# Attention of an adaLN layer with experts: q and k in two float32r parts, heads two by two in the halves of TensorE

## The chip, the cores and the metric

The kernel runs on one core of one Trainium2 chip. The metric is the device time of one execution in microseconds. TensorE is PE, its weight loads PEld, VectorE is DVE, ScalarE ACT, GpSimd POOL; SP issues most DMAs.

## The reference

One transformer layer on x of 2048 tokens by 256 numbers, float32. `sa, ca, ga, sb, cb, gb` are rows of 256 made from a vector c; of the experts only the sizes matter here.

```python
h = layernorm(x) * (1 + ca) + sa
qkv = h @ w_qkv.T + b_qkv                      # 16 heads of 16 numbers
scores = q @ k.T / 4 + causal                  # per head 2048 x 2048
out = softmax(scores) @ v
x = x + ga * (out @ w_out.T + b_out)
h = layernorm(x) * (1 + cb) + sb
x = x + gb * ffn(h)                            # top 1 of 8 experts, at most 320 tokens each, 256 -> 1024 -> 256
```

## The kernel before

**Tiles.** The 16 heads are four groups of four (g), the 2048 queries four blocks of 512 (b); n = 4 g + b counts 16 blocks. For each block the kernel needs the row maxima of the scores first, and then the transposed scores (keys by queries), whose exponentials are the weights of the values. So each product of q and k is formed twice. *Maxima*: for one head, one tile of 128 queries and one chunk of up to 512 keys a matmul (L1295) writes a PSUM bank and DVE reduces it (L1049); in the chunk with the diagonal DVE adds the causal mask and reduces in one instruction (L1055). *Scores*: for one head and one tile of 128 keys a matmul (L1325) writes 128 keys by up to 512 queries and ACT takes the exponential (L802). For the tiles on the diagonal only the later queries are formed (512, 384, 256 or 128 columns) and POOL zeroes the triangle (L698). *Weigh* (L1245): four heads' values by the exponentials of one tile of keys, float32, each head in its own 32 columns of the array, added up in one bank. A *step* here is one tile of keys: scores of its four heads, maxima of blocks to come, and the weigh of the tile before it; 160 steps in all.

**Precision.** q and k are float32 numbers split in three bfloat16 parts (L757, L762 on ACT, `leave_part0` and `leave_part1` on DVE or POOL). The six products that matter stand below each other in `stacks`: 6 x 16 = 96 rows. Eight more rows carry minus the row maximum in two bfloat16 parts (q side) and ones for the own head, zeros for the others (k side), so that the score matmul of 104 rows gives score minus maximum. The parts go through DRAM (`qk_rows`) to be laid out so: `store_parts` (six DMAs for a block) and `load_stacks` (two DMAs), all issued by SP in a fixed order. The projections of a group (L1187, float32, in four pieces) run between the steps of the group before; group 0 is made in the prologue.

**Maxima rows.** When the last maxima of a block are read, DVE forms the two parts (`max_parts`), PE turns them (L1302), ACT copies the eight rows to the first head's stack (L790) and signals (L793), and DVE copies them to the three others (L1075). The first score of the block waits for that.

**Order.** Each engine runs its instructions in order. `attention_plan` writes one list of events for all of them, with a clock of its own that says when a bank is free. Maxima use banks 0 to 2 in turn, scores banks 3 to 5, the weigh bank 6, everything else bank 7: a maxima matmul waits for the read three before it, a score for the exponential three before it:

```python
                    if u >= 3:
                        pe.wait_ge(max_read, u - 2)
                    q0 = b * QB + qt * P
```

When no maxima are left, steps of the output projection, second layernorm and gate for the first 12 token tiles (`tail_slot`) are put between the scores of the last two blocks.

## Time and profile before

| | |
|---|---|
| three runs | 782.13, 784.63, 785.97 us |
| median | 784.63 us |
| span of the profiled execution | 782.6 us, mean granted clock 0.943 |
| PE, DVE, ACT, POOL busy | 88, 72, 59, 17% |
| maxima, 640 matmuls | 197.7 us busy on PE |
| scores, 640 matmuls | 195.4 us busy on PE |
| weigh, 1280 matmul records | 151.6 us busy on PE |
| exponentials, 640 | 298.3 us busy on ACT |
| maxima read without and with mask, 384 and 256 | 250.7 and 120.7 us busy on DVE |

The page names one time for the profiled execution, its span. The time of a run is taken from the device and not from the trace. L numbers are lines of the kernel before. The busy time of PE is made of modelled ends, so matmuls that follow each other overlap in it. A float32 matmul stands in the trace as two records, one of bfloat16 or float32r as one. All events of attention lie before 594 us of the span; then come the last four token tiles, the scatter of the tokens to their experts and, from 633 us, the experts.

### The profile page before, as it was taken

To read this page: it belongs to the slowest core of one execution; us is meant where nothing else is said; L and a number is where in the kernel's file an instruction comes from. 1 tells how busy PE (TensorE), PEld (TensorE's weight loads), DVE (VectorE), ACT (ScalarE), POOL (GpSimd) and SP (SyncE) were. 2 spreads that over 40 slices of the span, in tenths; PEclk is the share of its full clock that TensorE was granted. 3 is DMA by queue.
4 is the path that set the end of the run, shared out by engine and by line. 5 is a ranking of instruction groups with operands and counts; after the bars stand their busy time and mean duration, and the time that the engine had idled before them with its cause. 6 is when DMAs were issued, how large, how long until landed. Compare 5 with 4: busy or idle time off the path is not lost.

```text
span 782.6 us, 12208 instructions
## 1 busy us (share of the span) xinstructions
PE 689.1 (88%) x4290; PEld 367.2 (47%) x4290; DVE 561.1 (72%) x1467; ACT 459.5 (59%) x962; POOL 133.9 (17%) x194
## 2 busy tenths in 40 slices
PE   4686989999999998999999999989996279999994
PEld 3564534432323343323332323242543269999994
DVE  7754778788888787988888898960435437777762
ACT  1422445566676667766677676657783336656551
POOL 6000222220001132003310201100105300121122
PEclk9869889999999999999999999999999559999998
DMA  7436126630006033005900006000004283455200
GB/s 243 109 76 144 41 57 147 162 68 14 2 0 162 1 81 81 2 1 124 308 1 1 1 1 214 1 28 1 28 28 162 90 234 115 155 182 201 92 23 17
DMA packets 42111, 66.53 MB, mean 85 GB/s; under 512 B 3822, under 2 KB 31985, under 8 KB 41466
## 3 DMA queue, kind: packets, MB, share of 16 engines
q1 hardware_dynamic: 39746, 59.44, 27.3%
q0 software_dynamic: 2304, 6.31, 2.2%
q8 instruction: 34, 0.56, 0.3%
q14 instruction: 27, 0.22, 0.1%
HBM read 39.36 MB, written 26.78 MB: 85 GB/s over the span
## 4 chain that ended last, share of the span: by engine, by line
PE 74%; DVE 10%; ACT 8%; issue 4%; DMA 2%; POOL 1%; SPq 0%; DVEq 0%; POOLq 0%; ACTq 0%
PE bank L1245 17%; PE bank L1295 15%; PE bank L1325 14%; PE bank L1430 9%; PE bank L1413 8%; ACT probs L802 4%; PE bank L1187 3%; DVE chunk_max L1049 2%; PE bank L1350 2%; PE bank L1216 1%; PE bank L1396 1%; ACT qk_sb L751 1%; PE bank L1373 1%; PE bank L1228 1%; DVE stats L907 1%
## 5 line engine op out<-in xcount | busy, mean ns | idle before, releaser
L802 ACT ACTIVATE probs<-bank 128x512 f32<-128x512 f32 (+3 forms) x640 | 298.3, 537 | 124.1 <-PE bank L1325 123.0
L1049 DVE TENSOR_REDUCE chunk_max<-bank 128x1 f32<-128x512 f32 x384 | 250.7, 685 | 36.9 <-PE bank L1295 35.9
L1325 PE MATMUL bank<-stacks 104*128 104x512 bf16 (+3 forms) x640 | 195.4, 356 | 13.5 <-ACT probs L802 10.1
L1295 PE MATMUL bank<-stacks 96*128 96x512 bf16 (+3 forms) x640 | 197.7, 359 | 7.9 <-DVE chunk_max L1049 3.2
L1245 PE MATMUL bank<-probs,v_sb 128*32 128x512 f32 (+3 forms) x1280 | 151.6, 546 | 0.1
L1055 DVE CUSTOM_DVE_ANT_0 masked<-bank,causal 128x128 bf16<-128x128 f32 (+3 forms) x256 | 120.7, 484 | 15.4 <-PE bank L1295 14.6
L1295 PEld LDWEIGHTS bank<-stacks 96*128 96x128 bf16 x640 | 56.0, 98 | 160.0 <-DVE chunk_max L1049 79.4
L698 POOL TENSOR_SCALAR_AFFINE_SELECT probs<-probs 128x512 f32<-128x512 f32 x64 | 40.6, 635 | 397.4 <-ACT probs L802 397.4
L1325 PEld LDWEIGHTS bank<-stacks 104*128 104x128 bf16 x640 | 62.2, 100 | 98.7 <-ACT probs L802 65.6
L1430 PE MATMUL bank<-w_split,acts 128*128 128x256 f32 x576 | 79.9, 284 | 0.0
L1430 PEld LDWEIGHTS bank<-w_split,acts 128*128 128x128 f32 x576 | 74.5, 190 | 1.5 <-issue 0.8
L1413 PE MATMUL bank<-slotT,w_split 128*128 128x320 f32 x384 | 70.0, 320 | 2.1 <-DVE slotT L1109 2.1
L1413 PEld LDWEIGHTS bank<-slotT,w_split 128*128 128x128 f32 x384 | 59.5, 196 | 3.1 <-issue 2.3
L862 ACT ACTIVATE acts<-bank 128x320 fp32r<-128x320 f32 x64 | 28.0, 438 | 55.4 <-PE bank L1413 55.4
L1139 DVE TENSOR_TENSOR acts<-act_raw,acts 128x320 fp32r<-128x320 f32 x64 | 31.4, 490 | 33.6 <-ACT act_raw L865 33.6
L1187 PEld LDWEIGHTS bank<-hT,w_qk_sb 128*128 128x128 f32 x256 | 40.7, 219 | 13.8 <-issue 9.1
L1098 DVE TENSOR_TENSOR w_split<-w_raw,w_split 128x1024 fp32r<-128x1024 f32 x32 | 38.9, 1224 | 10.6 <-ACT w_split L837 10.6
L731 POOL DMA_INDIRECT out<-down,slots_sb x24 | 23.6, 984 | 132.0 <-DVE down L1127 127.2
L1187 PE MATMUL bank<-hT,w_qk_sb 128*128 128x128 f32 x256 | 43.7, 309 | 2.7 <-ACT hT L771 2.7
L1245 PEld LDWEIGHTS bank<-probs,v_sb 128*32 128x32 f32 x1280 | 25.4, 108 | 44.0 <-issue 27.6
L751 ACT ACTIVATE qk_sb<-bank,b_qk_sb,qk_scale 128x512 f32<-128x512 f32 x16 | 12.4, 777 | 43.2 <-PE bank L1187 43.2
L837 ACT CAST w_split<-w_raw 128x1024 fp32r<-128x1024 f32 x32 | 33.3, 1049 | 0.0
(140 smaller groups left out, 533.6 us busy)
## 6 DMA issues: line engine op xcount, KB each, us to landing
stacks<-qk_rows SPq DMA_DIRECT2D x6, 1536.0 KB, 12.4
w_raw<-w_in SPq DMA_DIRECT2D x8, 1024.0 KB, 5.0
w_raw<-w_down SPq DMA_DIRECT2D x8, 1024.0 KB, 8.0
qk_rows<-part SPq DMA_DIRECT2D x32, 192.0 KB, 2.9
slot_rows<-empty SPq DMA_DIRECT2D x1, 5140.0 KB, 28.9
slots_sb<-slot_rows SPq DMA_DIRECT2D x8, 514.0 KB, 4.0
qk_rows<-part SPq DMA_DIRECT2D x32, 128.0 KB, 2.4
stacks<-qk_rows SPq DMA_DIRECT2D x8, 384.0 KB, 4.5
```

Of the source, the lines that this page charges most:

```text
L698: pool.affine_select(out=d, in_=d, compare_op=ALU.is_ge, fill=0.0, base=0, pattern=[[0, HG], [1, P]], channel_multiplier=-1).then_inc(diag ...
L802: act.activation(probs[:, s % 3, h, 0:width], bank[SCORE_BANKS[u % 3]][:, 0:width], ACT.Exp)\
L837: act.copy(chunk(w_split[e % 2][:, 0, :], c), chunk(w_raw[:, e % 2, :], c)).then_inc(w_high, 1)
L1049: dve.tensor_reduce(to, src[:, 0:QB], AX.X, ALU.max).then_inc(max_read, 1)
L1055: dve.tensor_tensor_reduce(out=masked[:, u % 3, 0:width], in0=src[:, 0:width], in1=causal[:, QB - width:QB], scale=1.0, scalar=NEG, op0=AL ...
L1098: dve.tensor_tensor(chunk(w_split[e % 2][:, 1, :], c), chunk(w_raw[:, e % 2, :], c), chunk(w_split[e % 2][:, 0, :], c).bitcast(F32), ALU.s ...
L1187: mm = pe.matmul(bank[MISC_BANK][:, at:at + width], w_qk_sb[:, k, g * P:(g + 1) * P], hT[:, k, b * QB + at:b * QB + at + width], start=(k ...
L1245: mm = pe.matmul(bank[VALUE_BANK][CT * h:CT * (h + 1), lo:QB], v_sb[:, kt, g * HG + h, :], probs[:, s % 3, h, 0:QB - lo], start=first, sto ...
L1295: pe.matmul(bank[MAX_BANKS[u % 3]][:, 0:width], stack(g, 0)[0:KR, h, q0:q0 + P], stack(g, 1)[0:KR, h, c * QB:c * QB + width], start=True, ...
L1325: pe.matmul(bank[SCORE_BANKS[u % 3]][:, 0:QB - lo], stack(g, 1)[0:KR + MR, h, kt * P:(kt + 1) * P], stack(g, 0)[0:KR + MR, h, b * QB + lo: ...
L1413: mm = pe.matmul(bank[n % 3][:, 0:CAP], w_split[e % 2][:, a, col:col + P], slotT[:, e % 2, b, k, :], start=(i == 0 and k == 0), stop=(i == ...
L1430: mm = pe.matmul(bank[DOWN_BANKS[st]][:, 0:D], acts[:, n % AR, a, st * P:(st + 1) * P], w_split[e % 2][:, b, col:col + D], start=(it == 0 ...
```

## The change

q and k are split in two float32r parts instead of three bfloat16 ones, three products instead of six: 48 rows, 56 with the maxima rows. Two heads then fit in the array, one in rows 0 to 63 and one in rows 64 to 127. Each event of maxima or scores is now a pair of heads: two matmuls, one in each half, into the two banks of one of three buffers, and one instruction of DVE or ACT that reads 128 x 2 x up to 512 numbers. Maxima and scores share the three buffers; the plan gives each event the buffer that its own clock has free first, and the event waits for the last reader of that buffer, whichever kind it was (`free_pair`). In the first block's maxima only buffer 0 is used. When no maxima are left, scores use buffers 1 and 2, and the tail work of the first 12 tiles banks 0 and 1 only. The causal mask is added on PE: four short bfloat16 matmuls (a shifted identity by a shifted mask) ahead of the pair. The maxima rows are copied by ACT to a buffer of their own and from there by two DMAs, issued by SP, to both halves of the array's rows; SP's order now follows the plan. The ones rows (k side), before four ACT instructions of 8 x 2048 (L780) and a DMA, are eight DMAs at the start. ACT rounds the high part straight from PSUM, and one subtraction gives the low part. Stores of parts are four DMAs for a block, loads four; their bytes are the same. The experts are untouched.

```diff
-PARTS_Q = [0, 0, 0, 1, 1, 2]
-PARTS_K = [0, 1, 2, 0, 1, 0]
+PARTS_Q = [0, 0, 1]
+PARTS_K = [1, 0, 0]
 KR = HD * len(PARTS_Q)
+HALF = P // 2
+PAIRS_OF_HEADS = HG // 2
 MR = 2 * HG
...
-    return [[(qt, h, c) for qt in range(TB) for h in range(HG) for c in range(b + 1)] for b in range(NB)]
+    return [[(qt, j, c) for qt in range(TB) for j in range(PAIRS_OF_HEADS) for c in range(b + 1)] for b in range(NB)]
...
+    def usable():
+
+        if not started:
+            return [0]
+        return [0, 1, 2] if count < len(maxima) else [1, 2]
+
+    def next_buffer():
+        return min(usable(), key=lambda i: free_at[i])
...
+        i = next_buffer()
+        plan.append(("max", count, g, b, qt, j, c, width, i))
+        tensor(width / TENSOR_RATE + (50 if c < b else 130), free_at[i])
+        vector = max(vector, now + READ_LATENCY) + 2 * width / VECTOR_RATE + VECTOR_FIXED
+        free_at[i] = vector + FREE_LATENCY
+        count += 1
...
+    freed_by = {}
+    held = [None, None, None]
+    exps = 0
+    for ev in plan:
+        if ev[0] == "max":
+            freed_by[ev] = held[ev[-1]]
+            held[ev[-1]] = ("max_read", ev[1] + 1)
+        if ev[0] == "scores":
+            exps += 1
+            freed_by[ev] = held[ev[-1]]
+            held[ev[-1]] = ("exp_done", exps)
+    exps_of_first = held[0]
...
+        pair_bank = [ctx.enter_context(nc.psum_tensor(f"pair{i}", [P, 2, QB], F32)) for i in range(4)]
+        bank = [pair_bank[i // 2][:, i % 2, :] for i in range(8)]
...
-        stacks = sb1("stacks", [P, 2, 2, HG, S], BF16)
+        stacks = sb1("stacks", [P, 2, 2, PAIRS_OF_HEADS, S], F32R)
...
-        STACK_DMAS = 2
-        STORES = 6
+        STACK_DMAS = 4
+        STORES = 4
+        ROW_DMAS = 2
...
+            def load_group(g):
                 sp.wait_ge(parts_stored, 16 * STORES * NB * (g + 1))
                 if g >= 2:
 
-                    sp.wait_ge(scored, HG * (last_step[(g - 1) * NB - 1] + 1))
+                    sp.wait_ge(scored, 2 * (last_step[(g - 1) * NB - 1] + 1))
                 load_stacks(g, slice(0, S), stacked[g])
+
...
+            sp.wait_ge(heads_marked, 1)
+            for r in range(2):
+                for a in range(2):
+                    for j in range(PAIRS_OF_HEADS):
+                        marks = head_rows[:, a, j, :].rearrange("p (c s) -> p c s", c=1)
+                        to = stacks[HALF * a + KR:HALF * a + KR + MR, r, 1, j, :].bitcast(F32)
+                        sp.dma_start(to.rearrange("p (c s) -> p c s", s=MARKS),
+                                     marks.broadcast_to([MR, S // MARKS, MARKS])).then_inc(ones_copied, 16)
+            stored, grouped = 0, 0
...
+                if ev[0] == "max_rows":
+                    n = ev[1]
+                    g, b = divmod(n, NB)
+                    sp.wait_ge(misc_read_a, misc_reads(misc_use[ev])[0] + 1)
+                    row = max_row[:, n % 2, :].bitcast(F32).rearrange("p (j s) -> p j s", j=1)
+                    for a in range(ROW_DMAS):
+                        rows = stack(g, 0)[HALF * a + KR:HALF * a + KR + MR, :, b * QB:(b + 1) * QB].bitcast(F32)
+                        sp.dma_start(rows, row.broadcast_to([MR, PAIRS_OF_HEADS, QB]))\
+                            .then_inc(max_rows[n % 2], 16)
...
+            eng.tensor_tensor(part[:, 1, :], qk_sb[:, :], part[:, 0, :].bitcast(F32), ALU.subtract).then_inc(done, 1)
...
                 act.activation(qk_sb[:, :], bank[MISC_BANK][:, :], ACT.Identity, bias=b_qk_sb[:, g:g + 1],
+                               scale=qk_scale[:, 0:1])
+                if n >= 1:
+
+                    act.wait_ge(parts_stored, 16 * STORES * n)
+                act.activation(part[:, 0, :], bank[MISC_BANK][:, :], ACT.Identity, bias=b_qk_sb[:, g:g + 1],
                                scale=qk_scale[:, 0:1]).then_inc(misc_read_a, 1)
                 act.wait_ge(misc_read_a, misc_reads(misc_use["project", g, b])[0] + 1)
-                if n >= 1:
-
-                    act.wait_ge(parts_stored, 16 * STORES * n)
-                act.copy(part[:, 0, :], qk_sb[:, :]).then_inc(part0_ready, 1)
-
...
-            def second_part(g, b):
-                n = g * NB + b
-                act.wait_ge(rest_ready_v if g == 0 else rest_ready_p, n + 1 if g == 0 else n + 1 - NB)
-                act.copy(part[:, 1, :], rest[:, :]).then_inc(part1_ready, 1)
...
-                    second_part(0, b)
-
-                    act.activation(stacks[KR:KR + MR, 0, 1, b, :], ones_b[KR:KR + MR, 0:1].broadcast_to([MR, S]),
-                                   ACT.Copy, scale=head_sel[KR:KR + MR, b:b + 1]).then_inc(ones_rows, 1)
...
-                    act.copy(stack(g, 0)[KR:KR + MR, 0, b * QB:(b + 1) * QB],
-                             bank[MISC_BANK][:, :].bitcast(BF16)[0:MR, 0:QB]).then_inc(misc_read_a, 1)
-                    act.wait_ge(misc_read_a, misc_reads(misc_use[ev])[0] + 1)
-                    act.copy(c_tmp[0:1, 1, 0:1], c_tmp[0:1, 0, 0:1]).then_inc(max_row0, 1)
+                    if n >= 2:
+
+                        act.wait_ge(max_rows[n % 2], 16 * ROW_DMAS * (n // 2))
+                    act.copy(max_row[:, n % 2, :], bank[MISC_BANK][:, :].bitcast(BF16)[0:MR, 0:QB])\
+                       .then_inc(misc_read_a, 1)
...
-                    act.activation(probs[:, s % 3, h, 0:width], bank[SCORE_BANKS[u % 3]][:, 0:width], ACT.Exp)\
+                    act.activation(probs[:, s % 3, 2 * j:2 * j + 2, 0:width], pair_bank[i][:, :, 0:width], ACT.Exp)\
...
-                        dve.tensor_reduce(to, src[:, 0:QB], AX.X, ALU.max).then_inc(max_read, 1)
-                    else:
-                        if u >= 3:
-                            dve.wait_ge(max_read, u - 2)
-                        if u == 0:
-                            dve.wait_ge(causal_ready, 1)
-                        dve.tensor_tensor_reduce(out=masked[:, u % 3, 0:width], in0=src[:, 0:width],
-                                                 in1=causal[:, QB - width:QB], scale=1.0, scalar=NEG, op0=ALU.add,
-                                                 op1=ALU.max, accum_out=to).then_inc(max_read, 1)
+                    dve.tensor_reduce(chunk_max[:, n % 2, first:first + 2, c], pair_bank[i][:, :, 0:width], AX.X, ALU.max)\
+                       .then_inc(max_read, 1)
                 if ev[0] == "max_parts":
...
-                    rows = stack(g, 0)[KR:KR + MR, :, b * QB:(b + 1) * QB]
-                    dve.wait_ge(max_row0, n + 1)
-                    dve.tensor_copy(rows[:, 1:HG, :], rows[:, 0:1, :].broadcast_to([MR, HG - 1, QB]))\
-                        .then_inc(max_rows, 1)
...
-                    if u >= 3:
-                        pe.wait_ge(max_read, u - 2)
+                    free_pair(ev)
                     q0 = b * QB + qt * P
-                    pe.matmul(bank[MAX_BANKS[u % 3]][:, 0:width], stack(g, 0)[0:KR, h, q0:q0 + P],
-                              stack(g, 1)[0:KR, h, c * QB:c * QB + width], start=True, stop=True).then_inc(max_scored, 1)
+                    if c == b:
+
+                        for at in (HALF, 0):
+                            for a in range(2):
+                                rows = slice(HALF * a, HALF * (a + 1))
+                                pe.matmul(pair_bank[i][:, a, width - P + HALF - at:width],
+                                          shifted_ident[rows, at:at + P], shifted_mask[rows, HALF:at + P],
+                                          start=(at > 0), stop=False, skip_group_check=True)
+                    for a in range(2):
+                        rows = slice(HALF * a, HALF * a + KR)
+                        mm = pe.matmul(pair_bank[i][:, a, 0:width], stack(g, 0)[rows, j, q0:q0 + P],
+                                       stack(g, 1)[rows, j, c * QB:c * QB + width], start=(c < b), stop=True,
+                                       skip_group_check=True)
+                    mm.then_inc(max_scored, 1)
...
-                    if u >= 3:
-                        pe.wait_ge(exp_done, u - 2)
-                    pe.matmul(bank[SCORE_BANKS[u % 3]][:, 0:QB - lo], stack(g, 1)[0:KR + MR, h, kt * P:(kt + 1) * P],
-                              stack(g, 0)[0:KR + MR, h, b * QB + lo:(b + 1) * QB], start=True, stop=True)\
-                        .then_inc(scored, 1)
+                            pe.wait_ge(ones_copied, 16 * 8)
+                    free_pair(ev)
+                    for a in range(2):
+                        rows = slice(HALF * a, HALF * a + KR + MR)
+                        mm = pe.matmul(pair_bank[i][:, a, 0:QB - lo], stack(g, 1)[rows, j, kt * P:(kt + 1) * P],
+                                       stack(g, 0)[rows, j, b * QB + lo:(b + 1) * QB], start=True, stop=True)
```

In the diff `freed_by[ev]` is the reader of the buffer that the event takes, found by going through the plan once.

The pieces of order below are of PE, in one and the same step late in block 7, from weigh to weigh. First before:

```order
L1295 MATMUL bank<-stacks 128x512 [waits max_read] x3
L1325 MATMUL bank<-stacks 128x512 [waits exp_done] x2
L1295 MATMUL bank<-stacks 128x512 [waits max_read]
L1325 MATMUL bank<-stacks 128x512 [waits exp_done] x2
L1295 MATMUL bank<-stacks 128x512 [waits max_read]
L1245 MATMUL bank<-probs,v_sb 32x512 [waits exp_done]
L1245 MATMUL bank<-probs,v_sb 32x512 x3
```

Then the same step in the changed kernel (L1388 scores, L1362 maxima, L1289 weigh):

```order
L1388 MATMUL pair<-stacks 128x512 [waits max_read]
L1388 MATMUL pair<-stacks 128x512
L1362 MATMUL pair<-stacks 128x512 [waits exp_done]
L1362 MATMUL pair<-stacks 128x512
L1388 MATMUL pair<-stacks 128x512 [waits max_read]
L1388 MATMUL pair<-stacks 128x512
L1362 MATMUL pair<-stacks 128x512 [waits exp_done]
L1362 MATMUL pair<-stacks 128x512
L1289 MATMUL pair<-probs,v_sb 32x512 [waits exp_done]
L1289 MATMUL pair<-probs,v_sb 32x512 x3
```

Five maxima and four scores have become two pairs of each, and every pair waits for a reader of the other kind.

The maxima rows on SP, in the changed kernel, around the load of group 2 (L668 maxima rows, L620 stacks, L608 and L613 stores of parts):

```order
L668 DMA stacks<-max_row 8x2x512 [waits misc_read_a]
L668 DMA stacks<-max_row 8x2x512
L668 DMA stacks<-max_row 8x2x512 [waits misc_read_a]
L668 DMA stacks<-max_row 8x2x512
L620 DMA stacks<-qk_rows 48x2x2048 [waits scored,parts_stored]
L620 DMA stacks<-qk_rows 48x2x2048 x3
L668 DMA stacks<-max_row 8x2x512 [waits misc_read_a]
L668 DMA stacks<-max_row 8x2x512
```

Before, the rows did not pass SP; on DVE the copy stood among the maxima reads (L1049, L1055):

```order
L1049 TENSOR_REDUCE chunk_max<-bank 128x1 [waits max_scored]
L1055 ISA masked,chunk_max<-bank,causal 128x128 [waits max_read,max_scored]
L1055 ISA chunk_max 128x1
L1075 COPY stacks<-stacks 8x3x512 [waits max_row0]
L1049 TENSOR_REDUCE chunk_max<-bank 128x1 [waits max_scored]
```

The copy has left DVE, and two DMAs of each block stand in SP's queue among loads and stores.

## Rows read from the trace of the kernel before

**Rows 1.** The page, part 1: busy us, share of the span, instructions.
```profile
PE 689.1 (88%) x4290; PEld 367.2 (47%) x4290; DVE 561.1 (72%) x1467; ACT 459.5 (59%) x962; POOL 133.9 (17%) x194
```

**Rows 2.** Stages: us, busy us (x) of PE, PEld, DVE, ACT, POOL, granted clock, DMA.
```profile
0.00:80.00 80.00, 52.14 (x232) 39.37 (x232) 48.67 (x172) 24.27 (x28) 12.39 (x47) 0.87 0.51 140
80.00:234.00 154.00, 143.88 (x841) 58.70 (x840) 127.16 (x333) 91.92 (x195) 28.49 (x32) 0.94 0.27 62
234.00:514.00 280.00, 268.30 (x1693) 93.08 (x1696) 242.30 (x619) 193.15 (x425) 47.66 (x68) 1.00 0.25 69
514.00:594.00 80.00, 72.81 (x468) 32.71 (x460) 29.00 (x117) 57.97 (x131) 5.93 (x9) 0.98 0.06 21
```

**Rows 3.** Waits, 80 to 516 us: us in total, times, longest.
```profile
ACT probs L802 <- PE bank L1325: 102.5, 118, 2.7
DVE chunk_max L1049 <- PE bank L1295: 35.9, 66, 2.8
```

**Rows 4.** Timeline (start us, us, engine): block 7, and one narrower weigh.
```profile
341.98 1.07 PE L1245 MATMUL bank<-probs,v_sb 128*32 128x512 f32 x8
...
345.19 1.07 PE L1245 MATMUL bank<-probs,v_sb 128*32 128x512 f32 x8
...
346.19 0.77 PE L1295 MATMUL bank<-stacks 96*128 96x384 bf16 x3
...
341.31 1.28 DVE L1049 TENSOR_REDUCE chunk_max<-bank 128x1 f32<-128x512 f32 x2
...
344.00 2.06 ACT L802 ACTIVATE probs<-bank 128x512 f32<-128x512 f32 x4 [1.03 <-PE bank L1325]
...
403.12 0.85 PE L1245 MATMUL bank<-probs,v_sb 128*32 128x384 f32 x8
```

**Rows 5.** Groups by form: xcount, busy us, mean ns of one, idle before.
```profile
L1049 DVE TENSOR_REDUCE chunk_max<-bank 128x1 f32<-128x512 f32 x384 | 250.7, 685 | 36.9 <-PE bank L1295 35.9
L802 ACT ACTIVATE probs<-bank 128x512 f32<-128x512 f32 x448 | 236.7, 602 | 95.1 <-PE bank L1325 94.3
...
L1055 DVE CUSTOM_DVE_ANT_0 masked<-bank,causal 128x256 bf16<-128x256 f32 x64 | 25.9, 417 | 3.7 <-PE bank L1295 3.6
...
L802 ACT ACTIVATE probs<-bank 128x256 f32<-128x256 f32 x64 | 20.2, 388 | 11.9 <-PE bank L1325 11.9
```

**Rows 6.** Timeline of the expert stage on PE, 660 to 664 us.
```profile
661.02 1.05 PE L1413 MATMUL bank<-slotT,w_split 128*128 128x320 f32 x6
...
662.96 1.05 PE L1413 MATMUL bank<-slotT,w_split 128*128 128x320 f32 x6
```

**Rows 7.** Timeline, 510 to 530 us: one score that ACT waited for.
```profile
511.66 0.38 PE L1325 MATMUL bank<-stacks 104*128 104x512 bf16 x1
...
512.08 0.60 ACT L802 ACTIVATE probs<-bank 128x512 f32<-128x512 f32 x1 [0.28 <-PE bank L1325]
```

**Rows 8.** Timeline of the prologue and of the first maxima rows.
```profile
56.48 1.99 ACT L780 ACTIVATE stacks<-ones_b,head_sel 8x2048 bf16<-8x2048 bf16 x1
...
78.30 0.57 ACT L790 COPY stacks<-bank 8x512 bf16<-8x512 bf16 x1 [11.39 <-PE bank L1302]
...
79.87 0.61 PE L1325 MATMUL bank<-stacks 104*128 104x512 bf16 x1 [0.54 <-DVE stacks L1075]
```

**Rows 9.** DMA issues: xcount, KB each, us to landing.
```profile
stacks<-qk_rows SPq DMA_DIRECT2D x6, 1536.0 KB, 12.4
...
qk_rows<-part SPq DMA_DIRECT2D x32, 64.0 KB, 2.5
```

**Rows 10.** Busy time in two short stretches of block 1, columns as in rows 2.
```profile
95.00:105.00 10.00, 7.20 (x34) 3.38 (x34) 9.26 (x25) 3.03 (x6) 1.15 (x1) 0.90 0.29 63
105.00:110.00 5.00, 5.00 (x25) 3.36 (x24) 2.45 (x6) 2.40 (x5) 1.78 (x2) 0.52 0.12 25
```

**Rows 11.** Timeline, PE, 540 to 550 us: two weighs in a row after the maxima.
```profile
543.25 1.06 PE L1245 MATMUL bank<-probs,v_sb 128*32 128x512 f32 x8
...
545.64 1.06 PE L1245 MATMUL bank<-probs,v_sb 128*32 128x512 f32 x8
```

305 lines of the change are left out of this document (165 added, 140 removed).

## The prediction

> **What bounds the kernel now.** The page's busy times come first [rows 1]: PE is busy for 88% of 782.6 us, DVE for 72%, ACT for 59%. That is an average, so the second view splits it by stage [rows 2]. The change touches only what lies before 594 us; the remaining 188.6 us (last tokens, experts) keep their instructions. From 80 to 514 us maxima and scores run beside each other: 154 us while the projections of two groups lie between them, then 280 us. There PE is busy for 93 to 96%, DVE for 83 to 87%, ACT for 60 to 69%. From 514 to 594 us no maxima are left. The third view is the waits [rows 3]: ACT waited 102.5 us for score matmuls, DVE only 35.9 us for maxima matmuls. The end of a matmul is modelled, so the fourth view is one step on the timeline [rows 4]. Weighs start at 341.98 and 345.19 us, a step of 3.21 us. The weigh holds PE until the next matmul at 346.19, 1.00 us; between weighs stand four scores and five maxima, nine matmuls of mostly 512 columns, each 213 ns at 2.4 GHz (granted 1.00): 1.92 us. PE streams 2.92 of 3.21 us. DVE is close behind: its 512-wide reads follow each other in 0.60 us, so five cost 3.0. ACT needs 2.06. So PE sets the step, and DVE would take over 0.2 us lower: halving PE's work cannot halve the time.
>
> **The new units.** 640 maxima become 320 pairs, 640 scores 320 pairs. Reading 1024 numbers at once: the 512-wide reduction takes 685 ns and 256 more columns cost 268 ns [rows 5], so alone it takes 685 + 536 = 1.22 us, and back to back 0.60 + 0.54 = 1.14 us, against 1.20 for two reads before. The exponential takes 602 ns at 512 and 388 at 256 [rows 5]: 602 + 428 = 1.03 us alone, and (2.06 - 0.60)/3 = 0.49 plus 0.43, 0.92 us, back to back.
>
> PE's price of a pair has no row, since no two row halves run at once before. The experts give a float32r matmul [rows 6]: six of 320 and nine of 256 columns in 1.94 us, where 4224 columns at 2.4 GHz are 1.76, so each costs its columns plus 12 ns. A pair of 512 columns then lies between 0.24 us (halves beside each other) and 0.45 us (one after the other). I take 0.25, as the weigh's rows are nearest: its eight records of 512 columns would be 1.71 us one after another even with one pass each, and took 1.00 [rows 4], so quarters of the array do run beside each other. That this holds for row halves in float32r is not shown.
> The Trainium skill (TensorE: Matmul & The Clock Gate, Part 3, packing small matmuls) has row tiles start about 4 ns apart; by it the pair is the lower bound, by its absence the sum below grows by the 48 us of the first rival.
>
> A diagonal maxima pair also gets its mask by four short bf16 matmuls, two by two: 192 columns, 80 ns; I take 0.1 us, 128 times, inside the steps.
>
> **The step after.** Three buffers serve both kinds, and a buffer is refilled only after its reader ends. From matmul start to ACT start is 0.42 us for 512 columns [rows 7], so the reader begins 0.21 us after the pair. In the order of block 7 (score, maxima, score, maxima, weigh) PE issues the score at 0, maxima at 0.25, score at 0.50, and the second maxima has to wait for the first score's buffer: 0.25 + 0.21 + 1.03 + 0.03 for the release = 1.52 (the 0.03 is my allowance). It ends at 1.77; the weigh (same four matmuls, 1.00 us) ends the step at **2.80 us** by rounding the buffer handover up. DVE's two reads need 2.3 of it. With a third maxima between, DVE is the limit of one read, and I take **3.0 us**. The same step before had 4.5 to 5 maxima.
>
> *234 to 514 us* (by the order 94 steps, blocks 4 to 13 and two of block 14). 60 full steps without projection, 44 with at most two maxima and 16 with more: 44 x 2.80 + 16 x 3.0 = 171. Four with a projection carry maxima of 18 full widths, which DVE reads in 18 x 1.14 = 21. Ten steps each of 384, 256 and 128 columns: 2.5, 2.1 and 1.5 us by the same walk, 61, less 13 because the weigh that follows is narrower. Heads out and turned, ten times 0.6: 6. Sum **246**, before 280: **-34**.
> *80 to 234 us* (39 steps): 22 full, 14 x 2.80 + 8 x 3.0 = 63; eight with a projection, maxima of 46 widths x 1.14 = 53; nine narrow ones 17 less 4; heads 4, and 4 for the rows of block 1, which come right before its first score: **137**, before 154: **-17**. Here PE's 1.7 us of a projection hides under DVE.
> *514 to 594 us*: scores have two buffers, ACT reads continuously: two exponentials back to back, 1.86 us, plus 0.1, against 2.39 [rows 11], for eleven plain steps: -5. The other steps carry the transposes, projections and gates of twelve token tiles; two pairs cost 0.5 us where four matmuls cost 0.85, for 13 steps -5, and the shared banks of the tail (0 and 1 only) give nothing back because DVE was waited for there anyway. **-10**.
> *Prologue*: four ACT instructions of 1.99 us that stood ahead of the next block's hT leave [rows 8], and one subtraction and one cast per block: about -6 on the path. The first eight maxima pairs now share one buffer, so PE and DVE alternate: 2 x (0.95 + 1.2 + 1.55 + 1.95) = 11.3 us against 5.6: +6. Maxima rows: before, ACT's copy starts at 78.30 and the first score at 79.87; now ACT's copy (0.57) is followed by two DMA issues on SP (0.6 each) and a landing of 2.5 us, the smallest store's [rows 9]: 4.3 instead of 1.6 us, +1 here since three maxima cover the rest. Later blocks are scheduled several us ahead. **+1**.
> SP's queue: rows stand behind stores and behind a 3 MB load whose halves land after 12.4 us [rows 9]. By the order at least eight score pairs, some 10 us, lie between them where they meet: nothing on the path. DVE's row copies and accumulator reads leave too; both are inside the read times above. POOL keeps one subtraction of two, off the path.
>
> Sum: 782.6 - 34 - 17 - 10 + 1 = 722.6. A stretch in which PE is paced by DVE lost clock before [rows 10]: granted 0.52 after ten us with PE busy for 72%. Five us at half clock delay PE by 2.5; with fewer columns I expect two such stretches more and add 5: **728 us**. The sum stands against the execution's 782.6; the median, 784.6, is 0.3% above, which is nothing beside the terms.
> The Trainium skill (TensorEngine Tiling (Array Packing), Key Properties) says that a change of tiling mode drains TensorE. The trace agrees: the weigh's 1.00 us exceed its streaming: 128 columns more cost 0.22 us, from 0.85 to 1.07 [rows 4], so 512 take some 0.87, and 0.13 is left. Before, only weighs changed mode; now each of 48 projection pieces between pairs does as well, an estimate of 6 us by half that drain each way, which the sum leaves out as DVE covers it.
>
> **Rivals.** (1) *The halves don't overlap.* A pair costs 0.45: the step becomes 0.45 + 0.21 + 1.06 + 0.45 + 1.00 = 3.17, +0.37 for 92 full steps, +0.25 for 42 narrow ones, +3 in the tail: **776 us**, about as before. For it: no row shows two row halves. Against: the weigh's quarters. (2) *The clock falls* (slower). PE streams 1.85 of 2.8 us instead of 2.9 of 3.2 and stands 0.8 us in each step. At 1.2 GHz pair and weigh double: 0.48 + 0.21 + 1.06 + 0.48 + 2.0 = 4.2 us, 1.4 more than at full clock. It decides from 55/1.4 = 39 of the 134 steps on; in 60 of them, **812 us**. For it: rows 10. Against: from 234 us on, with DVE waits in each step, the granted clock was 1.00 [rows 2]. (3) *Maxima rows late*: the DMA path 3 us exposed in each of 14 later blocks, **770 us**. For it, blocks of group 0 have only three or four pairs between rows and first score; against, the order gives later blocks several steps. (4) *DVE runs without gaps*: if the ring costs half of what I think, DVE's reads bound the two stages at 122 + 205 us; half way there from my 383 is 28 less: **700 us**.
>
> **How the numbers follow.** Forecast 0.60; (1) 0.12; (2) 0.08; (3) 0.08; (4) 0.12. The range 698 to 772 takes in the forecast with (3) and (4) and leaves out (1) and (2), 0.20. A measurement tells 0.5% (4 us) from no change. Faster takes the forecast, (3), (4) and some third of (1): 0.84; the rest of (1) is no change or slightly slower: same 0.07; slower, (2) and a little of (1): 0.09.
>
> **What would show it.** Weigh starts in block 7 some 2.8 us apart, PE idle before the second maxima pair and released by ACT; a pair's matmuls within 0.25 us; DVE reads of 1.22 us, busy 82 to 88%; granted clock above 0.9; first score near 81 us, last weigh near 536. A pair at 0.45 us, a clock near 0.5 in whole blocks, or waits of the score matmuls for max_row DMAs would prove it wrong.

## The result and the profile after

The changed kernel takes **847.34 us** (median of 4 runs, 843.95 to 849.8); the kernel before, on the same chip, 785.3 (4 runs, 782.13 to 790.99). The ratio is 1.079, 95% interval 1.074 to 1.085: slower by 8%, where I forecast 728 us and faster. Each ratio here and below rests on the runs within 1.5% of a kernel's fastest; a longer run is left out of it, while medians are over all runs. The profiled execution has a span of 844.6 us and a mean granted clock of 0.877 (before: 782.6 us, 0.943).

The page, against [rows 1]: every engine is busy for a smaller share, though PE's busy time in us is no smaller (692.3, before 689.1). The clock row shows a digit under 9 in 18 of its 40 slices.

```profile
PE 692.3 (82%) x4802; PEld 401.8 (48%) x4802; DVE 539.2 (64%) x871; ACT 425.6 (50%) x622; POOL 125.4 (15%) x186
...
PEclk9868569868899997699999977999997758999998
```

By stage, against [rows 2]; group 0 now ends at 272 us instead of 238, the last maxima at 563 instead of 507, attention at 655 instead of 594. What comes after attention takes 190 us, before 189.

```profile
80.00:272.00 192.00, 156.26 (x1060) 74.64 (x1064) 124.93 (x140) 88.44 (x115) 20.26 (x24) 0.81 0.26 55
272.00:563.00 291.00, 252.21 (x1916) 105.93 (x1912) 213.53 (x238) 172.62 (x216) 42.96 (x63) 0.91 0.19 33
563.00:655.00 92.00, 82.96 (x518) 39.16 (x510) 38.51 (x130) 57.96 (x83) 8.64 (x12) 0.91 0.37 128
```

The stages are too coarse to find 62 us in, so I took the start of each of the 160 weighs from the two timelines. Differences of these starts, from the last weigh of one block to the last of another (for block 15, up to the third last; where a later kernel weighs in two halves, the first half counts):

```
us, from weigh to weigh    before   after   difference
to the end of block 0       106.3   120.0      +13.7
block 1                      36.7    51.0      +14.3
block 2                      47.1    52.8       +5.8
block 3                      47.8    47.9       +0.1
blocks 4 and 5               32.3    30.7       -1.6
block 6 (4 projections)      47.6    64.8      +17.2
block 7                      46.0    46.8       +0.8
blocks 8 to 10               65.0    64.9       -0.1
block 11                     47.4    53.4       +6.0
blocks 12 and 13             31.1    30.2       -0.9
block 14                     40.8    39.7       -1.1
block 15                     40.8    48.5       +7.7
```

In the blocks without a projection, a load or a fall of the clock (7 to 10, 12 and 13) the two kernels are equal: 142.1 against 141.9 us. So two questions stand apart: why halving PE's work gives nothing there, and where the other 62 us come from.

**A plain step** at full clock, of block 7, on the timeline (start, us, engine, line, operation):

```profile
393.94 0.50 PE L1388 MATMUL pair<-stacks 56*128 56x512 f32 x2
394.28 0.40 PE L1362 MATMUL pair<-stacks 48*128 48x512 f32 x2
394.49 1.94 ACT L864 ACTIVATE probs<-pair 128x1024 f32<-128x1024 f32 x2 [1.12 <-PE pair L1388]
394.52 0.40 PE L1388 MATMUL pair<-stacks 56*128 56x512 f32 x2
394.73 1.23 DVE L1108 TENSOR_REDUCE chunk_max<-pair 128x2 f32<-128x1024 f32 x1 [0.71 <-PE pair L1362]
395.56 0.50 PE L1362 MATMUL pair<-stacks 48*128 48x512 f32 x2 [0.64 <-ACT probs L864]
396.00 1.06 PE L1289 MATMUL pair<-probs,v_sb 128*32 128x512 f32 x8
396.99 0.51 PE L1388 MATMUL pair<-stacks 56*128 56x512 f32 x2
```

It is the walk of the prediction: score, maxima, score, then PE waits, released by ACT, and the weigh. The starts give the prices. Inside a stream the next pair comes 0.24 us later (394.28 to 394.52), so the halves do run beside each other and rival 1 falls. But the first pair behind a weigh takes 0.34, the one ahead of a weigh 0.43 to 0.44. From the first score to the second maxima it is 1.62 us (I had 1.52), on to the weigh 0.44 (0.25), and the weigh 0.99: 3.05 instead of 2.80, against 3.21 before.

**The hole of block 2.** SP issues the 3 MB load of group 1 from 142.81 us, the maxima rows at 151.55; the first scores wait until 167.45, and ACT waits 10 us for a store behind the same load.

```profile
142.81 3.03 SPq L620 DMA_DIRECT2D stacks<-qk_rows  x4
151.55 1.70 SPq L668 DMA_DIRECT2D stacks<-max_row  x2
167.45 1.22 PE L1388 MATMUL pair<-stacks 56*128 56x512 f32 x4 [9.93 <-DMA stacks<-max_row]
167.93 0.78 ACT L827 ACTIVATE part<-pair,b_qk_sb,qk_scale 128x512 fp32r<-128x512 f32 x1 [10.02 <-DMA qk_rows<-part]
170.55 1.76 DVE L1108 TENSOR_REDUCE chunk_max<-pair 128x2 f32<-128x256 f32 x2 [11.63 <-PE pair L1362]
```

**A step with a projection** (block 6). Behind the projection PE issues a score, a maxima and a score pair (319.19 to 319.78). ACT first reads the projection twice, so two of three buffers stand full of scores; DVE has nothing for 1.5 us and PE waits until the first exponential is done. Behind the wait the clock falls: that pair takes 0.73 us instead of 0.50, and from 322 to 326 us the granted clock is 0.51.

```profile
319.30 0.78 ACT L822 ACTIVATE qk_sb<-pair,b_qk_sb,qk_scale 128x512 f32<-128x512 f32 x1 [4.76 <-PE pair L1231]
319.78 0.49 PE L1388 MATMUL pair<-stacks 56*128 56x512 f32 x2
319.98 0.77 ACT L827 ACTIVATE part<-pair,b_qk_sb,qk_scale 128x512 fp32r<-128x512 f32 x1
320.88 1.91 ACT L864 ACTIVATE probs<-pair 128x1024 f32<-128x1024 f32 x2
321.94 0.73 PE L1362 MATMUL pair<-stacks 48*128 48x512 f32 x2 [1.67 <-ACT probs L864]
322.70 1.23 DVE L1108 TENSOR_REDUCE chunk_max<-pair 128x2 f32<-128x1024 f32 x1 [1.52 <-PE pair L1362]
```

**The waits** from 80 to 655 us, against [rows 3]: DVE now waits 139.2 us for maxima (35.9 before), ACT 152.2 for scores (102.5). PE waited 10.1 us for ACT before, in 28 waits of at most 1.1 us; now it is 40.1, 20.8 of them at maxima pairs and 19.3 at the mask ahead of such a pair.

```profile
ACT probs L864 <- PE pair L1388: 152.2, 155, 5.1
DVE chunk_max L1108 <- PE pair L1362: 139.2, 185, 11.6
...
PE pair L1362 <- ACT probs L864: 20.8, 40, 1.7
...
PE pair L1388 <- DMA stacks<-max_row: 13.9, 4, 9.9
```

### The profile page after: what moved, and what is told of

It is laid out like the page before. It is cut to its first block, busy times and chain, and to the rows that moved or that the text cites. A ratio compares the mean times of both kernels' runs of the same rounds, so it can differ in the third digit from the quotient of the medians.

```text
span 844.6 us, 12055 instructions
## 1 busy us (share of the span) xinstructions
PE 692.3 (82%) x4802; PEld 401.8 (48%) x4802; DVE 539.2 (64%) x871; ACT 425.6 (50%) x622; POOL 125.4 (15%) x186
## 4 chain that ended last, share of the span: by engine, by line
PE 67%; ACT 12%; DVE 11%; DMA 4%; issue 4%; POOL 1%; SPq 0%; DVEq 0%; POOLq 0%
PE pair L1289 16%; PE pair L1388 10%; PE pair L1362 9%; ACT probs L864 9%; PE pair L1503 8%; PE pair L1486 7%; PE pair L1231 5%; DVE chunk_max L1108 4%; PE pair L1357 2%; DMA qk_rows<-part 2%; PE pair L1422 2%; PE pair L1260 1%; PE pair L1272 1%; PE pair L1446 1%; PE pair L1469 1%
## 5 line engine op out<-in xcount | busy, mean ns | idle before, releaser
L1108 DVE TENSOR_REDUCE chunk_max<-pair 128x2 f32<-128x1024 f32 (+3 forms) x320 | 334.8, 1064 | 147.3 <-PE pair L1362 144.7
L864 ACT ACTIVATE probs<-pair 128x1024 f32<-128x1024 f32 (+3 forms) x320 | 276.2, 893 | 154.7 <-PE pair L1388 152.2
L1289 PE MATMUL pair<-probs,v_sb 128*32 128x512 f32 (+3 forms) x1280 | 168.4, 600 | 0.6 <-ACT probs L864 0.6
L1388 PE MATMUL pair<-stacks 56*128 56x512 f32 (+3 forms) x640 | 148.1, 468 | 24.1 <-DMA stacks<-max_row 13.9
L1362 PE MATMUL pair<-stacks 48*128 48x512 f32 (+3 forms) x640 | 148.1, 472 | 24.0 <-ACT probs L864 20.8
L1388 PEld LDWEIGHTS pair<-stacks 56*128 56x128 f32 x640 | 64.1, 200 | 157.4 <-DVE chunk_max L1108 54.8
L1362 PEld LDWEIGHTS pair<-stacks 48*128 48x128 f32 x640 | 66.8, 212 | 54.6 <-ACT probs L864 38.9
L1503 PE MATMUL pair<-w_split,acts 128*128 128x256 f32 x576 | 79.9, 284 | 0.0
L1503 PEld LDWEIGHTS pair<-w_split,acts 128*128 128x128 f32 x576 | 74.4, 190 | 1.5 <-issue 0.8
L1486 PE MATMUL pair<-slotT,w_split 128*128 128x320 f32 x384 | 70.0, 320 | 2.1 <-DVE slotT L1153 2.1
L1357 PE MATMUL pair<-shifted_mask,shifted_ident 64*128 64x128 bf16 (+1 forms) x512 | 36.1, 225 | 26.2 <-ACT probs L864 19.3
L1231 PEld LDWEIGHTS pair<-hT,w_qk_sb 128*128 128x128 f32 x256 | 43.0, 246 | 21.8 <-issue 20.1
L1289 PEld LDWEIGHTS pair<-probs,v_sb 128*32 128x32 f32 x1280 | 26.6, 112 | 40.5 <-issue 32.5
L1357 PEld LDWEIGHTS pair<-shifted_mask,shifted_ident 64*128 64x128 bf16 x512 | 15.8, 101 | 56.9 <-ACT probs L864 31.9
```

The costliest lines, as they stand in the source:

```text
L864: act.activation(probs[:, s % 3, 2 * j:2 * j + 2, 0:width], pair_bank[i][:, :, 0:width], ACT.Exp)\
L1108: dve.tensor_reduce(chunk_max[:, n % 2, first:first + 2, c], pair_bank[i][:, :, 0:width], AX.X, ALU.max)\
L1231: mm = pe.matmul(bank[MISC_BANK][:, at:at + width], w_qk_sb[:, k, g * P:(g + 1) * P], hT[:, k, b * QB + at:b * QB + at + width], start=(k ...
L1289: mm = pe.matmul(bank[VALUE_BANK][CT * h:CT * (h + 1), lo:QB], v_sb[:, kt, g * HG + h, :], probs[:, s % 3, h, 0:QB - lo], start=first, sto ...
L1357: pe.matmul(pair_bank[i][:, a, width - P + HALF - at:width], shifted_ident[rows, at:at + P], shifted_mask[rows, HALF:at + P], start=(at > ...
L1362: mm = pe.matmul(pair_bank[i][:, a, 0:width], stack(g, 0)[rows, j, q0:q0 + P], stack(g, 1)[rows, j, c * QB:c * QB + width], start=(c < b), ...
```

## Experiments

The theories: *ring* (three shared buffers couple PE, DVE and ACT), *clock* (the pauses halve TensorE's clock), *rows and load* (DMAs behind a load), *mask*. Numbers of blocks below are differences of weigh starts as in the table. They went in four groups (e1 to e4, e5 to e8, e9 to e11, e12 to e14), each beside runs of the kernel before, whose medians were 782.6, 786.8, 787.1 and 784.7 us.

### e1: dummies ahead of the maxima that wait

```diff
+                    if open_block is not None and held_open >= 2:
+                        keep_busy(FILL)  # twice: bank 6 += zeros (128 x 128) by zeros (128 x 512), bf16
                     free_pair(ev)
```

> The changed kernel with two bf16 matmuls of 512 zero columns (zero weights, added to the open sum of the values) put ahead of each maxima pair that waits behind two score pairs; nothing else changes, and the sums stay what they are. Clock theory: in the changed kernel TensorE's granted clock stands at half for some 143 of the 575 us from 80 to 655 us against 23 of 514 before, because PE pauses in each step; with the pauses filled the clock holds, plain steps stay at 3.05 to 3.2 us, and the run is 20 to 40 us shorter than the changed kernel's 847. Ring theory (the three shared buffers alone set the step, the clock is only a symptom): no shorter than 840 us, or longer by up to 0.4 us in each of some 90 steps.

843.0 us, ratio 1.077 (1.069 to 1.084). From 200 to 560 us the granted clock is 0.99 instead of 0.91; block 6 falls from 64.8 to 56.1 us and block 11 from 53.4 to 49.0, but block 7, which had full clock anyway, grows from 46.8 to 49.0. The clock theory holds in its first half only: dummies hold the clock, and what they cost eats most of what it gives. 20 to 40 us was wrong; by the two ratios the gain is 0.3%, inside their intervals.

### e2 and e3: the rows on another queue; the load behind the rows

```diff
-                        sp.dma_start(rows, row.broadcast_to([MR, PAIRS_OF_HEADS, QB]))\
+                        act.dma_start(rows, row.broadcast_to([MR, PAIRS_OF_HEADS, QB]))\
```

> The changed kernel with the two maxima-row DMAs of each block issued on ACT's queue behind ACT's copy, not on SP's. Queue theory: the rows of block 2, issued at 151.55 us, waited 15 us because they stand in SP's queue behind a 3 MB load; on a queue of their own they land in about 4 us, the 11.6 us hole of DVE near 160 us goes, and the run is 8 to 15 us shorter than 847. Bandwidth theory: the load fills all 16 DMA engines, the rows land as late from any queue, and the time stays within 3 us of 847, plus up to 10 us because ACT now spends some 0.7 us on each of 32 issues.

866.3 us, ratio 1.104 (1.099 to 1.109): slower than the change by some 2%. The queue part is right, the longest wait for rows fell from 9.9 to 3.0 us and DVE's longest from 11.6 to 6.2. But each block now holds ACT for two issues behind its copy, 16 times, and ACT holds the buffers (the clock, too, stood at half for 172 us between 80 and 655 us, against 143 in the change):

```profile
389.61 1.46 ACTq L852 DMA_DIRECT2D stacks<-max_row  x2
...
391.82 0.50 PE L1360 MATMUL pair<-stacks 48*128 48x512 f32 x2 [1.46 <-ACT probs L862]
```

The Trainium skill (DMA: Bandwidth & Descriptors, Queues, rings and completion order) says that a DMA engine goes round the queues that have work, packet by packet. The shorter wait agrees with it.

```diff
-                        if stored == 1 or grouped >= stored - 1:
+                        if stored > 1 and grouped >= stored - 1:
                             load_group(stored)
...
+                    if n == 2:                         # behind the rows of block 2
+                        load_group(1)
```

> The changed kernel with the 3 MB load of group 1 issued behind the maxima rows of block 2 and not ahead of them (at about 153 and not 143 us; its first reader comes near 215 us). If the load is what holds the rows up, by either theory of the queue, the wait of 9.9 us of the first scores of block 2 shrinks to under 1 us and the run is 10 to 14 us shorter than 847; a clock that does not fall behind this hole (it stood at 0.5 from 163 to 180 us) would add 3 to 6 us more to the gain. If the hole only moves to the next wait, less than 5 us.

843.3 us, ratio 1.076 (1.070 to 1.081). The rows' wait is gone, block 1 falls from 51.0 to 44.5 us, and block 2 grows from 52.8 to 56.9: the hole only moved. Its waits from 140 to 200 us:

```profile
PE pair L1359 <- ACT probs L866: 14.0, 2, 12.5
ACT part L829 <- DMA qk_rows<-part: 11.1, 1, 11.1
```

ACT waits in order for the stores of the block before, which now stand behind the load, and with ACT the whole ring.

### e4: no mask on PE

```diff
-                    if c == b:
+                    if False:
```

> The changed kernel without the four short bf16 matmuls of the causal mask ahead of each of the 128 diagonal maxima pairs; the maxima are then taken over unmasked scores. My price was 0.1 us each on PE, inside the steps. Ring theory: 60 to 100 of the 128 stand on the chain that hands a buffer over, so 6 to 12 us shorter than 847. If PE had room for them, within 3 us of 847. If the mask on PE is a main cause of the loss, over 20 us shorter.

844.3 us, ratio 1.079 (1.073 to 1.085), as the change itself: taking the mask away gains nothing, so it is no main cause of the loss. That it costs nothing isn't shown. Block 3, at full clock in both, is 46.4 us against 47.9; but from 80 to 655 us this kernel stood at half clock for 173 us against 143, block 7 for 20 of its 53.4 us, and that can have eaten a gain of some us.

### e5 and e6: who holds PE, ACT or DVE

```diff
-                    act.activation(probs[:, s % 3, 2 * j:2 * j + 2, 0:width], pair_bank[i][:, :, 0:width], ACT.Exp)\
+                    some = max(P, width // 2)
+                    act.activation(probs[:, s % 3, 2 * j:2 * j + 2, 0:some], pair_bank[i][:, :, 0:some], ACT.Exp)\
```

> The changed kernel in which ACT takes the exponential of the first half of each row of scores only, and the weighing matmuls read that half twice (in a tile of 384 columns a third, three times); the instructions and columns of PE are unchanged. Ring theory: the second maxima pair of a step waits for the buffer of the step's first score pair, so the step is 1.62 (its handover with a 1.02 us exponential) + 0.44 + 0.99; with an exponential of about 0.6 us PE no longer waits there, full-clock steps of block 7 fall from 3.05 to 2.6 to 2.7 us, the block from 46.8 to some 43, the kernel by 30 to 50 us. DVE theory (its 1.22 us reads set the step): block 7 stays within 1 us of 46.8.

```diff
-                    dve.tensor_reduce(chunk_max[:, n % 2, first:first + 2, c], pair_bank[i][:, :, 0:width], AX.X, ALU.max)\
+                    dve.tensor_reduce(chunk_max[:, n % 2, first:first + 2, c], pair_bank[i][:, :, 0:width // 2], AX.X, ALU.max)\
```

> The changed kernel in which DVE takes the maxima of the first half of each row only; all else unchanged. DVE theory: the step follows DVE, so block 7 falls from 46.8 to under 43 us and the kernel by over 30 us. Ring theory: full-clock steps stay at 3.0 us since the buffer that PE waits for is ACT's, block 7 falls by at most 1.5 us, and the kernel by 5 to 12 us.

One run each: 806.0 us (span 804.3) and 829.8 (828.1). In e5 the second maxima of the step comes 1.19 us behind the first score and the weighs 2.61 apart; block 7 takes 43.3 us.

```profile
375.26 0.50 PE L1396 MATMUL pair<-stacks 56*128 56x512 f32 x2
376.45 0.51 PE L1370 MATMUL pair<-stacks 48*128 48x512 f32 x2 [0.21 <-ACT probs L865]
376.88 1.07 PE L1297 MATMUL pair<-probs,v_sb 128*32 128x512 f32 x8
379.49 1.06 PE L1297 MATMUL pair<-probs,v_sb 128*32 128x512 f32 x8
```

In e6 DVE's read is 0.69 instead of 1.23 us, and the weighs are 3.05 apart as ever, PE released by ACT; block 7 takes 47.3 us.

```profile
388.53 1.06 PE L1289 MATMUL pair<-probs,v_sb 128*32 128x512 f32 x8
388.64 0.69 DVE L1108 TENSOR_REDUCE chunk_max<-pair 128x2 f32<-128x512 f32 x1 [0.69 <-PE pair L1362]
391.14 0.51 PE L1362 MATMUL pair<-stacks 48*128 48x512 f32 x2 [0.53 <-ACT probs L864]
391.58 0.64 PE L1289 MATMUL pair<-probs,v_sb 128*32 128x512 f32 x4
```

This settles the ring: the step is the handover of ACT's buffer, the maxima pair, and the weigh, in a row. DVE isn't in it. Both kernels leave work out (half of the exponentials, half of the maxima) and serve only to tell which engine PE waits for. The whole of e6 gained 17 us by one run, more than the 5 to 12 expected: 7.5 of them in block 11, where the clock did not fall this time, 3.1 in block 6.

### e7: ACT reads the projection once

```diff
+                if n >= NB:
+                    act.activation(qk_sb[:, :], bank[MISC_BANK][:, :], ACT.Identity, bias=b_qk_sb[:, g:g + 1],
+                                   scale=qk_scale[:, 0:1]).then_inc(misc_read_a, 1)
+                    return
...
+                    pool.wait_ge(parts_stored, 16 * STORES * n)
+                    pool.tensor_copy(part[:, 0, :], qk_sb[:, :]).then_inc(part0_ready, 1)
                     low_part(pool, n, part1_ready_p)
```

> The changed kernel in which ACT reads each projection of groups 1 to 3 once (0.78 us) and GpSimd makes both parts from the copy in SBUF; ACT's second read of 0.77, its marker of 0.19 and its wait for the stores of the block before leave. Theory that ACT's reads lock the ring: in a step with a projection both score pairs stand in two of three buffers while ACT reads the projection for 1.74 us, so DVE idles some 2 us (1.97 at 321.94); the step loses 1 us, 12 times, block 6 falls from 64.8 by 4 to 8 us and the kernel is 8 to 15 us under 847. If these steps are long for the clock or for PE alone: within 3 us of 847.

828.7 us, ratio 1.055 (1.047 to 1.063): 2.4% of the time of before less than the change, somewhat more than expected. Block 6, the change and then e7:

```profile
302.00:367.00 65.00, 57.10 (x374) 28.47 (x372) 41.42 (x46) 28.89 (x40) 7.63 (x8) 0.79 0.20 51
```

```profile
297.00:349.00 52.00, 46.36 (x378) 23.66 (x377) 40.86 (x46) 25.28 (x32) 10.11 (x12) 0.97 0.25 64
```

The same DVE work in 13 us less. 4 x 0.97 us of ACT leave; the rest goes with the clock, 0.97 instead of 0.79. e3, which leaves this block's instructions as they are, bears that out: 58.8 us with 13 us at half clock, where the change took 64.8 with 26.5. The wait that ACT had for the stores behind the load now falls on GpSimd (19.2 us, once), and block 2 drops from 52.8 to 43.2 us; block 1, where PE still waits 12.4 us for the rows, takes 53.7.

### e8: weighs in two halves

```diff
+                if j == 0 and weigh is not None and weigh[2] == QB:      # planner: behind the first score pair
+                    fill(weigh[3])
+                    plan.append(("weigh", weigh[0], weigh[1], 0))
+                    tensor(560, weigh[3])
...
+                at, to = (lo, QB) if piece is None else (piece * QB // 2, (piece + 1) * QB // 2)
```

> The changed kernel with each weighing of 512 columns issued in two halves of 256 columns, the first behind the step's first score pair and the second behind the second, the planner told so. Ring theory: the 1.0 us of the weigh then lies in part beside the wait for the buffer instead of behind it; my walk with the traced durations gives block 7 44 instead of 47 us and 9 us less for the whole, and the clock falls less often, so 8 to 25 us under 847. Against it, by the rows of before 128 columns of a weigh cost 0.22 us of 1.07, so a half costs 0.63 and not 0.5: if PE is what limits, the split adds 0.2 us in each of some 130 steps and the run is 10 to 25 us longer than 847.

843.2 us, ratio 1.070 (1.061 to 1.079). Both halves of a block's first tile open the sum of the values here, which changes that sum; later kernels weigh that tile whole. Both sides were right somewhere: block 7 takes 42.5 us instead of 46.8, block 6 50.8, and the clock holds from 230 to 560 us but for one short fall. Block 1 takes 54.9 us; block 2 takes 59.8, 50 of them at half clock, and block 15 56.9, 29 at half clock (14 in the change). A half costs 0.57 us.

### e9, e10, e11: the repairs together

e9 is e7 with the load of group 1 in four parts; e10 adds the halves while maxima are left; e11 adds dummies at the start.

```diff
+                    if ev[1] == 1:                     # e9: columns of one block, behind its stores
+                        sp.wait_ge(parts_stored, 16 * STORES * (NB + ev[2] + 1))
+                        load_stacks(1, slice(ev[2] * QB, (ev[2] + 1) * QB), stacked[1])
...
                 if ev[0] == "gate_bias":
+                    pe.wait_ge(hT_ready, NB * DT)      # e11
+                    keep_busy(3, 16)
...
+                        if n < 2:                      # e11: ahead of the wait for the rows
+                            keep_busy(MISC_BANK, 8)
```

> e7 with the 3 MB load of group 1 in four parts, each behind the stores of its block, so that no row and no store stands behind more than 768 KB. e3 took the rows' wait away (block 1: 51.0 to 44.5 us) and gave it back because ACT then waited 11.1 us for stores behind the same load (block 2: 52.8 to 56.9). Theory that the load is the cause of both: block 1 at 43 to 46 us and block 2 at 42 to 48, the kernel 6 to 12 us under e7's 828.7. If the low clock after 160 us has causes of its own, block 1 stays over 48 us and the gain under 5 us.

> e9 with the weighings of 512 columns in halves while maxima are left, a block's first tile whole. In e8 the halves gave steps of 2.7 us (blocks 7 and 11 in 42 to 42.5 us, block 6 in 50.9) and a clock that held at 1.00 from 220 us on, but lost all of it in blocks 1, 2 and 15. Ring theory, clock included: blocks 4 to 13 give 20 to 25 us against e9, the kernel ends at 793 to 806 us. Counter-theory (the halves cost PE in steps with projections, so group 0 loses what the rest gains, as e8's 843 says): 815 us or more.

> e10 with dummy bf16 matmuls of zeros in the two places where PE stands longest while the clock falls: 16 of 512 columns ahead of the gate bias (PE idle 3.81 us to 79.23) and 8 ahead of the wait for the rows of blocks 0 and 1. Clock theory for the start: TensorE stands at 0.5 from 80 to 110 us because of these pauses; with them filled the clock holds to 110 us and the first weigh and block 0 come 5 to 10 us earlier. If the clock there falls for the many short waits between, or if the dummies only delay what follows: no gain, or up to 3 us loss.

e9: **816.6 us**, ratio 1.040 (1.033 to 1.047), 12 us under e7 as expected. Blocks 1 and 2 take 37.2 and 43.2 us (before: 36.7 and 47.1). Block 1 had 53.7 in e7, so there the load was the cause. Block 2 had 43.2 in e7 already, with the load in one piece: there it was enough that ACT no longer waits for the stores behind it.

e10: **795.4 us** median. Its ten runs lie between 779.6 and 833.6 us, with a granted clock from 0.92 down to 0.84, and the ratio of 0.996 (0.991 to 1.002) stands on the two fastest; by the median it is 1% slower than the kernel before. The middle went as expected, blocks 7 and 11 in 41.1 and 41.6 us, with nothing between the matmuls:

```profile
361.64 0.64 PE L1312 MATMUL pair<-probs,v_sb 128*32 128x256 f32 x8
362.21 0.49 PE L1412 MATMUL pair<-stacks 56*128 56x512 f32 x2
...
362.64 0.42 PE L1386 MATMUL pair<-stacks 48*128 48x384 f32 x2
...
362.99 0.64 PE L1312 MATMUL pair<-probs,v_sb 128*32 128x256 f32 x8
```

What varies is the start: in the profiled run the clock stood at 0.5 to 0.67 from 80 to 160 us.

e11: **776.0 us**, ratio 0.983 (0.975 to 0.991): faster than the kernel before, though one of its four runs took 802.3 us. Its stages:

```profile
80.00:115.00 35.00, 29.88 (x214) 15.70 (x214) 26.45 (x35) 9.87 (x14) 6.26 (x8) 0.90 0.39 85
115.00:300.00 185.00, 173.27 (x1626) 85.60 (x1624) 152.13 (x169) 110.29 (x135) 34.06 (x44) 1.00 0.34 71
...
490.00:585.00 95.00, 86.06 (x554) 40.44 (x552) 45.07 (x136) 57.30 (x81) 8.44 (x11) 0.89 0.36 126
```

Block 0 ends at 114.3 us instead of 124.2, block 1 takes 34.9 instead of 49.8 (36.1 and 51.0 by the second half of its last weigh): 25 us between the profiled runs. But e10's profiled run, 794.3 us, is 15 us over its fastest. The medians are 19 us apart, the fastest runs of the two (779.6 and 770.4 us) 9 and the ratios 1.3%, some 10 us, which is the safer figure for 32 dummies.

### e12, e13, e14: controls

> The changed kernel with e11's dummies at the start and nothing else of e7 to e11: 16 ahead of the gate bias, 8 ahead of the rows of blocks 0 and 1. In e11 they brought block 0's last weigh from 124 to 114 us and block 1 from 51.0 to 36.1, and the clock held at 1.00 from 80 to 160 us. Theory that the pauses of the start cost the clock by themselves: the kernel is 8 to 15 us under 847, block 0 ends at 110 to 114. Theory that the clock only holds where the ring is relieved too (halves, one read): it falls again by 110 us and the gain is under 5 us.

> The kernel before with dummies of 8192 columns in all ahead of its gate bias (PE idle there 3.81 us to 76.17 us), where its clock was 0.79, 0.70 and 0.66 in the tens of us at 70, 80 and 100. Clock theory: these stretches go to 1.00 and the kernel gains 2 to 6 us of 785, so e11's lead of 1.7% shrinks to about 1%. If its own stretches at half clock stand beside other waits (first parts, rows), within 2 us of 785.

> e11 with 8 more dummies (zeros added to the open sum of the values) ahead of the projection of token tile 5 and ahead of the expert counts, where PE waited 2.11 us to 524.90 and 2.22 us to 567.90 and the clock then stood at 0.5 to 0.6 for some 15 us. Clock theory: 2 to 6 us under e11's 776. Against it: the clock fell at 560 us already, before the second wait, so only one of the two can help and the dummies cost 1.7 us each where PE is not waiting: within 2 us of e11.

e12, the changed kernel with e11's dummies alone: 841.7 us, ratio 1.076 (1.070 to 1.082), by the ratios 0.3% under the change and inside the intervals. Block 0 ends at 123 us, block 1 takes 49.9. Under 5 us, as the second theory said: without the other repairs PE pauses again at once, and the clock (0.84 and 0.96 from 80 to 100 us) is at 0.55 in the next ten. The dummies are worth something only where PE has work without pauses behind them.

e13, the kernel before with as many dummy columns ahead of its gate bias as e11 has there: 783.2 us, ratio 0.998 (0.994 to 1.002), no difference; block 0 ends at 104 us instead of 106, and the clock still stands at 0.85 and 0.66 in the tens of us at 80 and 100. So the lead of e11 and e14 isn't that of the first dummies: by the medians, e14 against e13, beside the same runs of the kernel before, is 773.0 / 783.2 = 0.987.

e14, e11 with 16 more dummies in the tail: 773.0 us, ratio 0.985 (0.980 to 0.990), against e11's 0.983: no difference. The clock fell here too, from 554 to 568 us. e14 has the narrower interval and is the one to name: **1.5% faster than the kernel before**. One of its six runs took 806.4 us at a granted clock of 0.89, so a single execution can still lose; with that run in, the mean is 0.9% under that of the kernel before.

## Why the prediction was wrong

**The units.** DVE's 1.22 us is exact, ACT's 1.03 within 0.01:

```profile
L1108 DVE TENSOR_REDUCE chunk_max<-pair 128x2 f32<-128x1024 f32 x222 | 269.3, 1224 | 87.4 <-PE pair L1362 85.4
L864 ACT ACTIVATE probs<-pair 128x1024 f32<-128x1024 f32 x224 | 221.9, 1021 | 122.1 <-PE pair L1388 120.3
```

PE's 0.25 us for a pair was the price in a stream, and in the walk no pair that counts stands in a stream. Beside a weigh it costs 0.34 to 0.44. The kernel before had a little of this already: a single score costs 0.22 us in a stream and 0.31 ahead of a weigh. The rule that I cited from the Trainium skill (TensorEngine Tiling (Array Packing), Key Properties), that a change of tiling mode drains TensorE, is a possible reason, since the extra 0.1 to 0.2 us stands at each change; I counted it for the projections only. No run separates it from a weight load that nothing covers.

**The step after, 2.80 us.** The mechanism was right, with the waiting engine, its releaser and the place; its terms, 2.77 before I rounded up, were 0.28 us short, 0.19 of them on the maxima pair ahead of the weigh and 0.10 on the handover (1.62 for 1.52). That took the gain: 3.05 against 3.21, given back in the steps beside narrow weighs and turned heads (3.17 to 3.54 in block 7, before 2.84 to 3.09). "-34" for the plain stage was 0 at full clock and +11 as measured.

**Projections, "-17" and "DVE covers it".** This step failed outright. I let DVE's reads cover PE's 1.7 us and never put ACT's reads of the projection, 1.74 us, into a ring where scores hold two buffers meanwhile. "Covers" did hold while the pieces run: in block 6 a maxima pair and a projection piece take 0.44 + 0.64 us of PE (315.95 to 317.03), under DVE's 1.23. It failed behind the last piece. Block 6 lost 17.2 us of the 62 there, and e7 gives back 12.8 of them, the clock that follows the waits included. Blocks 1 and 2 lost 20.1 more; most of that lies with the load, in the next step.

**SP's queue, "nothing on the path".** Failed: I counted score pairs between load and rows, at full pace, instead of asking when the load's last byte lands. It cost a wait of 9.9 us on PE, and at the same time one of 10.0 on ACT for stores, which I had not listed as a waiter at all. e9 shows the first (block 1: 53.7 to 37.2 us), e3 that either wait alone keeps the hole, and e7 that block 2 recovers once ACT doesn't wait for stores.

**Clock, "+5".** Rival 2, at 0.08, happened in part, beside the other steps. From 80 us to the end of attention the clock stood at half for 143 us, before for 23. What that costs can be read where the instructions are the same and only the falls differ: block 11 takes 53.4, 51.2 (e7) and 48.1 us (e12) with 20.5, 13.7 and 3.4 us at half clock, 0.31 us for each; block 6 takes 64.8 and 58.8 (e3) with 26.5 and 13.0, 0.44 for each. The 120 us more are then an estimate of 37 to 53 us, more than half of the 62, though a fall that lies beside another wait costs less. Rival 2 had priced it at 84. My argument against it, that [rows 2] show 1.00 in spite of waits in each step, compared kernels in which it was DVE that waited, and not PE.

**Prologue, "+1"; tail, "-10".** The first score came at 84.97 us, 5.1 late: 3.1 of these at the gate bias (79.23 for 76.17) and 2.0 in rows and pauses. From there to the end of block 0 it took 35.0 us, before 26.4; 32 of them lay at half clock, before 9, and e11, with its other repairs and 7 at half clock, took 26.5. The plain steps of the tail came as forecast, 1.94 to 2.02 us at full clock (594 to 602 us; forecast 1.96, before 2.40). In block 15 each pair stands alone between work of another kind and costs 0.43 us of PE (617.64 to 618.07, 618.88 to 619.32). Two pairs then take 0.87, where I took 0.5, and four matmuls before took 0.97. The pieces between them got dearer: a gate 0.47 for 0.37, an output projection 0.96 for 0.86. PE has no pause here. The step takes 3.96 us where a step before took 3.42 (555.18 to 558.60), but it also holds four such pieces and not three.

```profile
617.64 0.51 PE L1388 MATMUL pair<-stacks 56*128 56x512 f32 x2
618.07 0.61 PE L1446 MATMUL pair<-w_gate_sb,part 128*128 128x8 f32 x4
...
618.54 0.42 PE L1409 MATMUL pair<-ident,token 128*128 128x128 f32 x2
618.88 0.50 PE L1388 MATMUL pair<-stacks 56*128 56x512 f32 x2
...
619.32 1.13 PE L1422 MATMUL pair<-w_o_sb,qk_sb 128*128 128x256 f32 x4
```

The kernel before, in such a step:

```profile
556.41 0.51 PE L1373 MATMUL bank<-w_gate_sb,rest 128*128 128x8 f32 x4
556.78 0.38 PE L1325 MATMUL bank<-stacks 104*128 104x512 bf16 x1
...
557.43 1.03 PE L1350 MATMUL bank<-w_o_sb,qk_sb 128*128 128x256 f32 x4
558.29 0.38 PE L1325 MATMUL bank<-stacks 104*128 104x512 bf16 x1
```

The other part of block 15's 7.7 us is the clock, which stood at half from 629.2 to 642.9 us and before not at all in this block: at 0.31 us each an estimate of 4 us. e10, with 6.8 us at half clock there, takes 46.9 us, e11 with 13.7 takes 48.8.

Of the rivals, (1) was wrong, (3) was right about one block in fifteen, (4) never came near: DVE was busy for 65 to 73% of the stages to 563 us, not 82 to 88.

**What stays open.** How the loss splits between waits and clock, beyond the estimate above: they come together, and e1 and e12, which fill pauses and leave the ring as it is, gain 4 to 6 us by their medians and 0.3% by the ratios, inside the intervals. Why the clock fell in one plain stretch (block 11) and not in blocks 7 to 10, with the same steps, no run shows. No run tells the drain from the weight load. In block 15 the 7.7 us are read from rows, not tried; e10, e11 and e14 still have them (46.9 to 49.4 us).

## What to carry to other kernels

Before PE's work is halved, walk the ring of buffers with each engine's whole queue in it, the rare readers too: with three shared buffers the step was one engine's read, one pair and the weigh in a row, and ACT, busy for only 64% of the step, held the other two. Cutting the long uninterruptible piece in two (the weigh, 1.0 us into two of 0.57) was worth more than the halving of matmuls: 46.8 to 41.1 us in block 7. And an edit that gives the bounding engine pauses changes the price of all its work; count the pauses it makes, not only the columns it saves.

## What the runs showed of the hardware

Two row halves of TensorE in float32r run beside each other: pairs of 512 columns follow each other in 0.24 us, where single bfloat16 matmuls of 512 columns before did in 0.22. A 1024-wide reduction over two banks of PSUM takes DVE 1.224 us, an exponential 1.021 on ACT. The rows' DMAs of 32 KB, behind a load of 3 MB on one queue, took 15.9 us from issue until their reader ran, from another queue the reader waited 3.0 us at most, not 9.9. The clock isn't fixed by the program: e10 gave 780 to 834 us in ten runs of the same work, the granted clock going from 0.92 down to 0.84 with it. The Trainium skill (TensorE: Matmul & The Clock Gate, A second HAM failure mode: psum-queue depth-cycling) describes this: PE idles briefly between groups of matmuls while it cycles through PSUM buffers, and the clock swings between its two levels. The trace agrees in the swing: 0.91 in the mean from 272 to 563 us, in stretches of 1.00 and of 0.5, with waits of 0.5 to 2 us in each step. But the waits alone don't decide it: blocks 7 to 10 have them too (0.64 us at 395.56) and kept 1.00 throughout.
